# Attention with gated experts on one core: the output projection in four parts of two pairs

## The reference

```python
xn   = layernorm(layernorm(x)) * gamma + beta
q    = xn @ w_q;  k, v = split(context @ w_kv)            # 16 heads of 64
attn = softmax(q * 64**-0.5 @ k.T)
a    = (attn @ v) @ w_out + b_out
x    = x + tanh(g_xattn) * tanh(gate) * a                 # called x1 below
t    = layernorm(x)
p    = softmax(t @ gate_w);  e = argmax(p)                # top-1 routing, 160 places an expert
y    = relu(t @ w1[e]) @ w2[e]                            # tokens past place 160 get nothing
out  = x + tanh(g_ffn) * p[e] * y
```

## Time and profile before

| | |
|---|---|
| median of three runs | 463.63 us |
| the profiled execution, its own time | 464.19 us |
| its span, first to last instruction | 462.1 us |
| mean granted TensorE clock | 0.988 |
| PE busy | 432.6 us, 94% |
| ACT busy | 381.7 us, 83% |
| DVE busy | 368.9 us, 80% |
| POOL busy | 355.7 us, 77% |

### The profile page before, as it was taken

How to read it: one execution, slowest core, us unless ns; L and a number is a source line. 1 busy time by engine, 2 the same in 40 slices (tenths; PEclk the granted TensorE clock), 3 DMA queues, 4 the chain that set the end, 5 groups by cost and what they waited for, 6 DMA issues and landing times.

```text
span 462.1 us, 13098 instructions
## 1 busy us (share of the span) xinstructions
PE 432.6 (94%) x5096; PEld 334.2 (72%) x5096; DVE 368.9 (80%) x803; ACT 381.7 (83%) x616; POOL 355.7 (77%) x270
## 2 busy tenths in 40 slices
PE   7887989999999999999999999999999999978993
PEld 6655757877777777776777777777777677757892
DVE  4788877799988898799879998899889887884622
ACT  5896979989988998899898998899889988981330
POOL 3686887788888897988888888898798887851325
PEclk9998999999999999999999999999999999989998
DMA  5998999999999999999999999999998999899111
GB/s 171 337 179 176 182 200 171 175 172 195 169 192 202 175 199 181 201 166 193 181 188 187 192 185 170 195 187 179 198 171 163 190 175 173 137 211 258 47 37 47
DMA packets 279964, 82.09 MB, mean 178 GB/s; under 512 B 264387, under 2 KB 276339, under 8 KB 279904
## 3 DMA queue, kind: packets, MB, share of 16 engines
q1 hardware_dynamic: 278528, 77.96, 94.8%
q0 software_dynamic: 1376, 3.30, 2.2%
HBM read 10.83 MB, written 5.14 MB: 35 GB/s over the span
## 4 chain that ended last, share of the span: by engine, by line
PE 65%; DVE 18%; ACT 8%; DMA 3%; issue 3%; POOL 2%; POOLq 0%; SPq 0%; ACTq 0%; DVEq 0%
DVE MXL L914 7%; PE psO L1295 5%; PE psO L1297 5%; PE psCD L1270 5%; PE psO L1296 5%; PE psAB L1263 4%; ACT P L757 4%; PE psCD L1263 4%; PE psAB L1270 3%; PE psEF L1191 3%; PE psEF L1193 3%; PE psEF L1192 3%; PE psEF L1310 3%; DVE HL L901 3%; PE psO L1356 3%
## 5 line engine op out<-in xcount | busy, mean ns | idle before, releaser
L660 POOL TENSOR_TENSOR PARTS<-P,PARTS 128x1024 f16<-128x1024 f32 x125 | 267.0, 2143 | 50.7 <-ACT PARTS L767 50.4
L767 ACT ACTIVATE PARTS<-P 128x1024 f16<-128x1024 f32 x126 | 135.2, 1073 | 0.8
L1295 PEld LDWEIGHTS psO<-VH,PT 128*128 128x128 f16 x1008 | 91.4, 98 | 21.2 <-issue 13.5
L1295 PE MATMUL psO<-VH,PT 128*128 128x65 f16 x1008 | 100.0, 196 | 3.0 <-DMA PT<-PARTS 1.6
L757 ACT ACTIVATE P<-psAB,NB 128x512 f32<-128x512 f32 x128 | 81.7, 698 | 25.1 <-DVE NB L917 24.9
L1296 PE MATMUL psO<-VL,PT 128*128 128x64 f16 x1008 | 99.3, 193 | 0.0
L1297 PE MATMUL psO<-VH,PT 128*128 128x65 f16 x1008 | 99.1, 194 | 0.0
L1296 PEld LDWEIGHTS psO<-VL,PT 128*128 128x128 f16 x1008 | 92.3, 99 | 0.1
L1297 PEld LDWEIGHTS psO<-VH,PT 128*128 128x128 f16 x1008 | 92.3, 98 | 0.0
L914 DVE TENSOR_REDUCE MXL<-psAB 128x2 f32<-128x1024 f32 x64 | 78.3, 1223 | 13.5 <-PE psAB L1263 6.7
L757 ACT ACTIVATE P<-psCD,NB 128x512 f32<-128x512 f32 x128 | 81.7, 701 | 1.9 <-DVE NB L917 1.0
(11 more groups left out here) (245 smaller groups left out, 858.9 us busy)
## 6 DMA issues: line engine op xcount, KB each, us to landing
ctx_raw<-in_ctx_dram SPq DMA_DIRECT2D x8, 256.0 KB, 4.1
w1s<-in_L_ffn_w_dram SPq DMA_DIRECT2D x8, 256.0 KB, 6.6
w2s<-in_L_ffn_w_dram SPq DMA_DIRECT2D x8, 256.0 KB, 4.6
PT<-PARTS SPq DMA_TRANSPOSE x126, 5.2
experts_table<-zeros POOLq DMA_DIRECT2D x2, 645.0 KB, 5.8
X<-in_x_dram SPq DMA_DIRECT2D x8, 128.0 KB, 3.4
wraw<-in_L_xattn_w_kv_dram SPq DMA_DIRECT2D x4, 256.0 KB, 4.9
out_dram<-row SPq DMA_DIRECT2D x8, 128.0 KB, 2.6
```

What stands on the lines that cost most here:

```text
L660: pool.tensor_tensor(PARTS[:, par, qt, 1], P32[:, par, qt], PARTS[:, par, qt, 0], ALU.subtract).then_inc(plo_done, 1)
L767: act.activation(PARTS[:, hp % 2, qt, 0], P32[:, hp % 2, qt], ACT.Copy).then_inc(phi_done[qt], 1)
L1295: pe.matmul(psO[:, g:g + DH + 1], phi, VH[:, kt, head, 0:DH + 1], start=first_, stop=False)
```

## The change

- The output projection is made in four parts of two pairs instead of two of four: pairs 0 and 1 in slot 5 and pairs 2 and 3 in slot 7 of the same sequence, pairs 4 and 5 in slot 1 and pairs 6 and 7 in slot 3 of the next. Each of the first three is added to X1 by an `add_part`, so there are three of them a sequence instead of one.
- In the last sequence the first two parts come in slots 5 and 7 too; behind the slots only pairs 4 and 5, and 6 and 7, are left.
- The values of the last pair go through psX (V's bank) instead of psO.
- The statistics of x1 move on DVE from the end of slot 3 to slot 4, behind the second row maximum; their end on GpSimd moves behind slot 4's first subtraction.
- In slot 2 (from sequence 1 on) the high part of tile 0's weights is made behind tile 1's exponentials.
- The gates' product and the scaled b_out are made by GpSimd, in slot 3 of sequence 0; the add of the bias moves from slot 7 to slot 4.

```diff
+        def exps_together(j):
+            return j >= PAIRS and j % PAIRS == CTX_STEP
-        PART_STEP, CTX_STEP, PROJECT_STEP = 1, 2, 3
+        CTX_STEP, PROJECT_STEP, MOMENTS_STEP = 2, 3, 4
+        PART_STEPS = {5: (0, 0), 7: (0, 1), 1: (1, 2)}
+        PARTS_A_BATCH = 3
+        def part_of(b, hp):
+            late, n = PART_STEPS.get(hp, (0, None))
+            return None if n is None or b < late else (b - late, n)
+        def part_pairs(n):
+            return range(2 * n, 2 * n + 2)
-        BO_STEP, BIAS_STEP = 2, 7
+        BO_STEP, BIAS_STEP = 3, 4
...
# GpSimd, a slot
+                    if is_first(b) and hp == BO_STEP:
+                        pool.wait_ge(tgate_done, 1)
+                        pool.tensor_tensor(gscale[:], tgates[:, 0:1], tgates[:, 1:2], ALU.mult).then_inc(gscale_done, 1)
+                        pool.wait_ge(gscale_done, 1)
+                        pool.wait_ge(bo_in, 16)
+                        pool.tensor_scalar(bo[:], bo[:], gscale[:, 0:1], None, ALU.mult).then_inc(bo_scaled, 1)
-                    if hp == PROJECT_STEP + 1 and not is_first(b):
-                        token_rstd(b - 1)
-                        token(b - 1, 0)
...
+                        if qt == 0 and hp == MOMENTS_STEP and not is_first(b):
+                            token_rstd(b - 1)
+                            token(b - 1, 0)
...
# ACT, a slot
-                    if j < LAST:
+                    if j < LAST and not exps_together(j):
                         phi(b, hp, 0)
                     exps(b, hp, 1)
+                    if j < LAST and exps_together(j):
+                        phi(b, hp, 0)
...
# DVE, a slot: behind both row maxima, ahead of kq_lo and normalise_heads
+                    if hp == MOMENTS_STEP and not is_first(b):
+                        token_moments(b - 1)
                     if j == LAST:
                         low_parts()
+                    if part_of(b, hp):
+                        add_part(*part_of(b, hp))
+                    if j == LAST:
                         place(B - 2)
-                    if hp == PART_STEP and not is_first(b):
-                        add_part(b - 1, b - 1)
                     if hp == PROJECT_STEP and not is_first(b):
                         add_attention(b - 1)
...
-                    if hp == PROJECT_STEP and not is_first(b):
-                        token_moments(b - 1)
...
-                    if is_first(b) and hp == BO_STEP:
-                        dve.wait_ge(tgate_done, 1)
-                        dve.tensor_tensor(gscale[:], tgates[:, 0:1], tgates[:, 1:2], ALU.mult).then_inc(gscale_done, 1)
+                    if is_first(b) and hp == BO_STEP + 1:
                         dve.wait_ge(gscale_done, 1)
-                        dve.wait_ge(bo_in, 16)
-                        dve.tensor_scalar(bo[:], bo[:], gscale[:, 0:1], None, ALU.mult).then_inc(bo_scaled, 1)
...
# PE, a slot: behind the K and Q projections, ahead of the V projection
-                    if hp == PART_STEP and not is_first(b):
-                        project_part(b - 1, range(PAIRS // 2))
+                    if part_of(b, hp):
+                        project_part(*part_of(b, hp))
...
# PE, behind all slots
                     values(b, PAIRS - 3)
-                    project_part(b, range(PAIRS // 2), psX)
-                    values(b, PAIRS - 1)
+                    values(b, PAIRS - 1, psX)
                     o_transposes(LAST - 2)
                     values(b, PAIRS - 2)
                     pe.wait_ge(route, (B - 2) * ROUTE + 7)
-                    project_part(b, range(PAIRS // 2, PAIRS - 2), psEF)
+                    project_part(b, PARTS_A_BATCH - 1, psEF)
```

More of the change, by code:

```diff
@@ L743, in ot_copy @@
                 if b:
-                    act.wait_ge(part_psum if pair < PAIRS // 2 else proj_psum, b)
+                    if pair < PAIRS - 2:
+                        act.wait_ge(part_psum, PARTS_A_BATCH * (b - 1) + pair // 2 + 1)
+                    else:
+                        act.wait_ge(proj_psum, b)
                 act.activation(OT[:, QT * pair:QT * (pair + pairs), :], bank.rearrange("p (t c) -> p t c", c=P),
@@ L917, in row_max, with normalise_heads @@
                 dve.tensor_reduce(NB[:, par, qt, :], MXL[:, par, qt], AX.X, ALU.add).then_inc(bias_done, 1)
-            def normalise_heads(b, hp):
+            def normalise_heads(b, hp, bank=psO):
                 j = b * PAIRS + hp
-                sums = psO[:, 0:2 * QT * (DH + 1)].rearrange("p (g d) -> p g d", d=DH + 1)
+                sums = bank[:, 0:2 * QT * (DH + 1)].rearrange("p (g d) -> p g d", d=DH + 1)
                 n = turn(j)
                 dve.wait_ge(pv_done, n)
+                if j == LAST:
+                    dve.wait_ge(norm_done, n - 1)
                 dve.reciprocal(rden[:, hp % 2, :], sums[:, :, DH]).then_inc(rden_done, 1)
@@ L937, in add_attention @@
                 dve.wait_ge(proj_psum, b + 1)
-                dve.wait_ge(part_done, B + 1 if is_last(b) else b + 1)
+                dve.wait_ge(part_done, PARTS_A_BATCH * (b + 1))
                 if b >= 2:
@@ L949, in add_attention, with add_part @@
                                          op1=ALU.add).then_inc(x1_done, 1)
-            def add_part(b, part, bank=psO):
+            def add_part(b, n, bank=psO):
+                part = PARTS_A_BATCH * b + n
                 dve.wait_ge(part_psum, part + 1)
@@ L1122, in _ @@
             normalise_heads(B - 1, PAIRS - 3)
-            add_part(B - 1, B - 1, psX)
-            normalise_heads(B - 1, PAIRS - 1)
+            normalise_heads(B - 1, PAIRS - 1, psX)
             normalise_heads(B - 1, PAIRS - 2)
-            add_part(B - 1, B, psEF)
+            add_part(B - 1, PARTS_A_BATCH - 1, psEF)
             add_attention(B - 1, [psX, psEF[:, 0:512]])
@@ L1272, in scores, with values @@
                 last.then_inc(score_psum, 1)
-            def values(b, hp):
+            def values(b, hp, bank=psO):
                 j = b * PAIRS + hp
                 par = hp % 2
-                wait_o((norm_done, turn(j)))
+                (wait_x if bank is psX else wait_o)((norm_done, turn(j)))
                 if j == 0:
@@ L1294, in values @@
                             first_, last_ = kt == 0, kt == KT - 1
-                            pe.matmul(psO[:, g:g + DH + 1], phi, VH[:, kt, head, 0:DH + 1], start=first_, stop=False)
-                            pe.matmul(psO[:, g:g + DH], phi, VL[:, kt, head, :], start=False, stop=False)
-                            last = pe.matmul(psO[:, g:g + DH + 1], plo, VH[:, kt, head, 0:DH + 1], start=False,
+                            pe.matmul(bank[:, g:g + DH + 1], phi, VH[:, kt, head, 0:DH + 1], start=first_, stop=False)
+                            pe.matmul(bank[:, g:g + DH], phi, VL[:, kt, head, :], start=False, stop=False)
+                            last = pe.matmul(bank[:, g:g + DH + 1], plo, VH[:, kt, head, 0:DH + 1], start=False,
                                              stop=last_)
@@ L1344, in last_transposes, with project_part @@
                 last.then_inc(p_psum, 1)
-            def project_part(b, pairs, bank=psO):
+            def project_part(b, n, bank=psO):
+                pairs = part_pairs(n)
                 if bank is psO:
-                    wait_o((part_done, b + 1))
-                elif bank is psX:
-                    wait_x((part_done, b + 1))
+                    wait_o((part_done, PARTS_A_BATCH * b + n + 1))
                 pe.wait_ge(ot_done, b * PAIRS + pairs[-1] + 1)
@@ L1393, in project @@
                     dst = psO[:, D * qt:D * qt + D]
-                    for pair in range(PAIRS // 2, PAIRS):
-                        last = pe.matmul(dst, OT[:, pair * QT + qt, :], wo[:, pair, :], start=(pair == PAIRS // 2),
+                    for pair in range(PAIRS - 2, PAIRS):
+                        last = pe.matmul(dst, OT[:, pair * QT + qt, :], wo[:, pair, :], start=(pair == PAIRS - 2),
                                          stop=(pair == PAIRS - 1))
```

3 lines of the change are left out of this document (2 added, 1 removed).

## The result

The changed kernel takes 474.59 and 475.39 us against 463.94 (median of four runs, 463.38 to 464.5): the ratio is 1.0261, 95% interval 1.0222 to 1.03, **slower**. The profiled execution's own time is 474.59 us.

The account below looks back on a forecast made before the run. PE was taken as the bound, with DVE right behind it. Six sequences +7.8, the last +0.3, the first +2.3, the tail -2.4: +8.0 on 463.63, told as 471.5 us; range 460.5 to 477 (the forecast's own 466 to 477).

Parts of the forecast that it names:

- the tail: Behind the last slots: PE loses a part of pairs 0 to 3 and a wait for psO; -2.4 us.
- The loop: Steady sequences: gains in slots 1, 3 and 4, losses in slots 5 and 7; +1.3 us each, +7.8 in six.
- Slot 5: DVE, late from the moved statistics, ends its second bias and the new add late, delaying `values`; +1.35 us.
- Slot 7: The new add behind DVE's second bias delays `values`, with no DVE lateness needed; +1.0 us.
- The mark that the prediction named for itself: Sign of being right: slots 5 and 7 over 7 and 6.5 us, PE idle before `values` for the add.
- its mark of being wrong: Sign of being wrong: `values` following the V projection at once in slots 5 and 7.
- The first sequence: Sequence 0: the gate stall in slot 3 goes, but PE waits for `wo` in slot 5; +2.3 us.
- The last sequence: The last pass through the slots: the loop's terms without slot 7's cost; +0.3 us.
- PE sets the pace everywhere: Rival: DVE runs ahead in slots with a part, so `values` waits for PE alone; 457 us, chance 0.17.
- GpSimd late as well: Rival: bias and statistics' end delay slot 4's subtractions and transposes, another 0.8 us a sequence; 477 us, chance 0.12.
- what I cost at nothing: GpSimd's moved bias and statistics' end, ACT's copies of transposed attention: no cost; uncovered, each under 0.8 us a sequence.
- A draw: Rival: DVE not late in slot 5, slots 1, 3 and 4 give all they can; 464.1 us, chance 0.13.

Follow-up runs that it names:

- e6: The changed kernel with the high part of tile 0's weights in slot 2 ahead of tile 1's exponentials again; 473.12 us, ratio 1.0208.
- e5: The changed kernel without DVE's adds of slots 5 and 7 in sequences 0 to 6, PE still multiplying those parts; 474.53 us, ratio 1.024.
- e7: The changed kernel with x1's statistics back in their old places on DVE and GpSimd; 479.26 us, ratio 1.032.
- e3: The changed kernel with the eight loads of the second expert weights issued behind those of the routed rows; 472.26 us, ratio 1.0182.
- e1: The kernel before with only the gates' product and the scaled b_out moved to GpSimd; 463.72 us, ratio 0.9992.
- e9: The changed kernel without the parts of slots 5 and 7 in sequences 0 to 6, on PE and DVE; 463.0 us, ratio 0.9979.
- e4: The changed kernel with two parts of four pairs again in sequences 0 to 6; 470.07, 468.59 and 473.36 us, ratio 1.0137.

## Why the prediction was right, and where it was not

The time was right (471.5 told, range 460.5 to 477; 474.59 and 475.39 measured), and three of the four terms are near. The fourth, the tail, came out the other way: it missed by 3.6 us, more than the 1.9 by which the span's +9.9 exceeds the sum's +8.0.

**The loop, +1.3 a sequence: measured +1.2.** Slot 1: -0.24 (-0.3 told). Slot 3: -0.21 (-0.2), and the exchange of the exponentials costs 0.35 (e6), where 0.4 was taken. Slot 4: -0.57 (-0.55). Slot 5: +1.55 (+1.35). Slot 7: +0.95 (+1.0). Slot 0 also gave 0.26, which I had not counted. DVE's first row maximum of slot 5 starts 1.62 into the slot (1.67 told), `values` at 5.93 (5.97 told).

The reasons were less right than the sum. The text hung slot 5 on the add behind the second bias, and said that without DVE's lateness it would cost +0.85. The add carries 0.06 of it (e5), and without the lateness it costs 1.30 (e7: 7.22 - 5.92). What was missing is psO's other user in that slot: PE's part cannot start before DVE has copied the transposed tokens out, 3.86 into the slot even with DVE on time (258.46 + 0.41 - 255.01 in e7). From there part and V projection, 0.91 and 0.85, lead to 5.68. Two chains of nearly one length ended the slot, and I had priced one. In slot 7 the same: PE's part carries 0.78 of the 0.95, the add 0.17 (e5). The mark that the prediction named for itself, PE idle before `values` for the add, stands in neither slot, and its mark of being wrong, `values` right behind the V projection, stands in both. For slot 5 that mark told the truth: the 5.97 came so near because the chain that was left out is as long as the one that was priced, which is luck. For slot 7 the add is in part the cause, and the mark was too coarse.

**The first sequence, +2.3: measured +1.9.** The step was right, `wo` late next, and the nearness is in part luck: e3, e6 and e7, whose sequence 0 is the same code, show +3.0, +2.4 and +4.0. `wo` was issued at 46.50, by the prediction's sum 45.9, and took 4.6 to land instead of 6.1, so PE was released at 51.20, where 52.0 was told; `values` of slot 5 started at 54.33, told 54.4. The gate instructions took 0.19 and 0.62 on GpSimd, 0.81 together, told 1.0. That the operations themselves were slow is out: DVE needs 0.34 for an instruction of the second's kind and size at the end of the kernel before (L978, a TENSOR_SCALAR of 128x128), where the earlier trace rows have 2.26. The Trainium skill ("SBUF — State Buffer", "Who interferes with whom") has the port pair that DVE and GpSimd share as an exclusive lock. The traces agree: the 3.8 us of the earlier trace rows shrank to 0.81, and slot 3 lost the stall in the changed kernel and in e1. But little of the won time is kept: e1's ten runs show no gain, and 4.4 us of waits for transposed blocks stand in its trace.

**The tail, -2.4: measured +1.2. This step failed.** The text said: "All of this is on PE's line, and nothing else is late". PE won 3.86, more than told; 1.66 of that lie in a stretch that ran at a lower clock before (last section), and the rest is near the 2.4. But the loads of the routed rows stand in SP's queue behind eight others and come 20 us behind the last slot's start whatever PE does. In the kernel before, they were there just when PE came (427.37 in the trace, against work that began at 427.41), so there was no wait to read. PE paid 3.42 for the wait and some 1.5 in the slower clock behind it. e3 turns the tail's +1.2 into -2.34, the told size, by that queue alone.

**The last sequence, +0.3: measured -0.1.** Its slots 0, 1, 3 and 4 gave 1.74 together, and slots 5 and 6 took 1.28 and 0.31.

**The rivals.** *PE sets the pace everywhere* (457) was a worse rival than its 0.17: even with those parts taken out the loop stays at 49.8 (e9), since transposed blocks are late next. *GpSimd late as well*: in the changed kernel PE waits only 0.9 us for transposed blocks, so it did not make this time. But the mechanism is there, 1.8 us of lateness that the long slots 5 and 7 cover: with the parts of these slots out it holds slot 7 in e9, and e4 has most of its waits in the same slot. The prediction's "what I cost at nothing" holds only under that cover. *A draw* had slot 5 at +0.85; no run's median came under +1.3 with the part in it.

What stays open: whether the loop could go under some 49.5 us with PE's parts out and GpSimd's work in its old places, or whether the queue of the transposes holds it there. No run tried the first, and none changed the transposes.

## What to carry to other kernels

Where work moves into a slot, list every user of the bank that it needs in that slot, and price the chain through each: two chains of one length hide one another, and removing one (here the add) then gains nothing. For each microsecond that PE is to win, look up in the DMA queue when its next operand lands: a load that arrives just as it is used shows no wait, and is the next bound. Before an engine's loop is shortened, take work out of it once: if the time stays, as in e9, the pace is set elsewhere, and the place of the waits that are left says where to look. And an edit that costs nothing under cover, as GpSimd's new order here, is priced again when the cover goes.

## What the runs showed of the hardware that was not expected

- The clock in the tail. In the stretch 411 to 419 of the kernel before, 4 to 12 us behind the start of the last slot, the granted clock was 0.79, with PE busy 6.84 of 8 us; in the changed kernel it stayed at 1.00 through the same stage (419.8 to 427.8), with PE busy 6.95. From the first transposes of the last pair's weights to the last matmul of the `values` behind them, the same work, PE took 5.96 us before and 4.30 after: this 1.66 is what PE's line won beyond the told 2.4, and a little more. The windows, and the second of the two sets of transposes, before and after:

```profile
411.00:419.00 8.00, 6.84 (x80) 6.54 (x81) 5.78 (x15) 3.58 (x6) 2.27 (x3) 0.79 1.08 226
```

```profile
419.80:427.80 8.00, 6.95 (x165) 6.48 (x163) 6.36 (x18) 3.86 (x6) 2.27 (x3) 1.00 1.04 225
```

```profile
413.25 1.97 PE L1343 MATMUL psCD<-ident,P 128*128 128x128 f32 x8 [1.00 <-ACT P L757]
...
421.73 1.09 PE L1368 MATMUL psCD<-ident,P 128*128 128x128 f32 x8 [0.88 <-ACT P L781]
```

- Transposes back to back: in e9 SP's queue issued eight in 21.63 us, 2.70 each, with 0.04 to 0.18 between them. Two to a slot make 5.4 us, little less than the shortest slots:

```profile
253.71 21.63 SPq L502 DMA_TRANSPOSE PT<-PARTS  x8
```
